# Two attention layers on one core: in layer 2, five low parts move to VectorE, the last blocks run in halves, and the score row is spread three blocks earlier

## The reference, cut to what matters

```python
def _L0_gnn_ref(xx_anchor, input, adj, weight):      # layer 1: masked attention over `input`
    anchor_adj = jnp.einsum('md,de,ne->mn', xx_anchor, weight, input)
    scores = jnp.where(adj > 0, anchor_adj, NEG_PAD)
    return jax.nn.softmax(scores / TEMPERATURE, axis=1) @ input

def _L1_gnn_ref(mole_out, adj, W, a1, a2):           # layer 2: additive attention
    Wh = mole_out @ W
    e = jax.nn.leaky_relu((Wh @ a1)[:, None] + (Wh @ a2)[None, :], negative_slope=0.2)
    att = jax.nn.softmax(jnp.where(adj > 0, e, NEG_INF), axis=1)
    return jax.nn.elu(att @ Wh)

x = _layernorm(x + _L0_gnn_ref(x, L0_gnn_input, adj, L0_gnn_weight))
x = _layernorm(x + _L1_gnn_ref(x, adj, L1_gnn_W, L1_gnn_a1, L1_gnn_a2))
```

## Time and profile before

| | us |
|---|---|
| median of 3 runs | 1453.31 (1448.89 to 1453.78) |
| the profiled execution, whole | 1454.16 |
| its span in the trace | 1452.1 |
| PE busy | 1414.8 (97%) |
| DVE busy | 1257.9 (87%) |
| POOL busy | 1212.2 (83%) |
| ACT busy | 1069.5 (74%) |

### The profile page before, as it was taken

The page is one execution under the profiler, slowest core; times in us unless marked ns, Lnnn a source line. Parts: engine busy times, 40 slices in busy tenths (PEclk is TensorE's granted clock), DMA queues, the critical chain, the costliest instruction groups (busy, mean ns, idle before and its releaser), DMA issues.

```text
span 1452.1 us, 28336 instructions
## 1 busy us (share of the span) xinstructions
PE 1414.8 (97%) x9663; PEld 1012.1 (70%) x9663; DVE 1257.9 (87%) x2136; ACT 1069.5 (74%) x2433; POOL 1212.2 (83%) x899
## 2 busy tenths in 40 slices
PE   8899999999999999999999999979999999999995
PEld 4577777777777777777777777765666666666664
DVE  6999999999999899999999999849898898979794
ACT  6788888888888888888888888868655555545453
POOL 6788888888888888888888878738999999999995
PEclk9999999999999999999999999998999999999998
DMA  8999999999999999999999998663534343434320
GB/s 263 290 269 265 266 262 258 262 270 273 270 271 258 265 259 259 274 270 271 273 257 264 260 256 266 188 138 72 103 66 110 79 102 87 102 70 110 74 58 14
DMA packets 427918, 291.38 MB, mean 201 GB/s; under 512 B 356864, under 2 KB 403200, under 8 KB 427776
## 3 DMA queue, kind: packets, MB, share of 16 engines
q1 hardware_dynamic: 427776, 289.59, 73.0%
HBM read 160.56 MB, written 40.89 MB: 139 GB/s over the span
## 4 chain that ended last, share of the span: by engine, by line
PE 95%; DVE 3%; issue 1%; ACT 1%; DMA 0%; POOL 0%; ACTq 0%; DVEq 0%; SPq 0%; POOLq 0%
PE ps L622 17%; PE ps L708 13%; PE ps L701 12%; PE ps L648 11%; PE ps L624 9%; PE ps L661 8%; PE ps L660 8%; PE ps L659 8%; PE ps L685 6%; PE ps L592 1%; PE ps L719 1%; DVE rows L974 1%; DVE neg_mask L949 1%; PE ps L585 0%; DVE pT_lo L983 0%
## 5 line engine op out<-in xcount | busy, mean ns | idle before, releaser
L833 ACT ACTIVATE rows<-rows,exp_bias 128x512 f32<-128x512 f32 x576 | 417.6, 725 | 57.0 <-DVE exp_bias L1033 57.0
L533 POOL TENSOR_TENSOR p_lo<-p,p_hi 128x1024 fp32r<-128x1024 f32 x180 | 423.7, 2392 | 23.1 <-ACT p_hi L869 11.9
L974 DVE CUSTOM_DVE_ANT_0 rows<-ps,neg_mask 128x1024 f32<-128x1024 f32 x288 | 352.1, 1222 | 79.9 <-PE ps L661 72.5
L1068 DVE SCALAR_TENSOR_TENSOR p<-ps,e_col,edgesT 128x1024 f32<-128x1024 f32 x288 | 349.7, 1275 | 53.2 <-PE ps L678 36.7
L440 POOL TENSOR_SCALAR edges<-neg_mask 128x1536 uint8<-128x1536 bf16 x190 | 307.4, 1618 | 97.0 <-DVE neg_mask L949 85.1
L869 ACT CAST p_hi<-p 128x1024 fp32r<-128x1024 f32 x180 | 185.1, 1047 | 167.7 <-DVE p L1068 165.1
L622 PE MATMUL ps<-vals,pT_hi 128*128 128x256 f16 x1536 | 296.2, 274 | 1.4 <-ACT att L812 0.9
L819 ACT CAST pT_hi<-ps 128x512 f16<-128x512 f32 x384 | 222.8, 580 | 92.1 <-PE ps L648 91.9
L482 POOL TENSOR_TENSOR inp_sb<-rows,inp_sb 128x512 f16<-128x512 f32 x192 | 281.5, 1486 | 9.6 <-ACT inp_sb L827 1.9
L624 PE MATMUL ps<-vals,pT_lo 128*128 128x128 f16 x1536 | 275.6, 220 | 0.0
L983 DVE TENSOR_TENSOR pT_lo<-ps,pT_hi 128x512 f16<-128x512 f32 x384 | 250.7, 683 | 12.5 <-ACT pT_hi L819 12.5
(11 more groups left out here) (119 smaller groups left out, 1857.1 us busy)
## 6 DMA issues: line engine op xcount, KB each, us to landing
adj_sb<-adj SPq DMA_DIRECT2D x192, 768.0 KB, 5.4
edge_rows<-edges SPq DMA_DIRECT2D x192, 192.0 KB, 4.8
xq<-x SPq DMA_DIRECT2D x48, 64.0 KB, 2.9
xr<-x SPq DMA_DIRECT2D x48, 64.0 KB, 5.5
out<-y_w SPq DMA_DIRECT2D x5, 512.0 KB, 3.5
inp_sb<-inp SPq DMA_DIRECT2D x3, 768.0 KB, 8.2
inp_sb<-inp_sb SPq DMA_TRANSPOSE x96, 4.6
edgesT<-edge_rows SPq DMA_TRANSPOSE x48, 5.5
```

The lines of the kernel that those rows point to most:

```text
L533: nc.gpsimd.tensor_tensor(p1_lo[:, m % LO_SLOTS, :], p1[:, (NB * g + n) % P_SLOTS, :], p1_hi[:, m % HI_SLOTS, :].bitcast(F32), ALU.subtrac ...
L833: nc.scalar.activation(row_chunk(1 - par, c), row_chunk(1 - par, c), ACT.Exp, bias=exp_bias[:, 1 - par:2 - par], scale=EXP_SCALE, accum_ou ...
L974: nc.vector.tensor_tensor_reduce(row_pair(par, k), scores_pair(k), neg_mask_row[:, 2 * k * CHUNK:2 * (k + 1) * CHUNK], 1.0, -3.0e38, ALU.a ...
L1068: nc.vector.scalar_tensor_tensor(out=p1[:, (NB * g + n) % P_SLOTS, :], in0=ps[:, R_ROW:R_ROW + 2, :].rearrange("p b w -> p (b w)"), scalar ...
```

## The change

1. **Five low parts by DVE** (`DVE_LOWS` = 25, 28, 33, 38, 43, in groups 1 to 5). For these blocks ACT copies `p1` to PSUM (`copy_rows`) ahead of its high part, and DVE subtracts (`low_rows`), three blocks later in its own order (`DVE_LAG`). Block 28 was split before, with its low part on POOL; 25, 33, 38 and 43 were plain and are now split. So a group has 34 split blocks, 29 of them with POOL, and 14 plain ones. In group 0 the five blocks are plain, which makes 28 plain there. Their values are split at the end of group 0 (5 small copies on ACT, 5 small subtractions on DVE). `p1_hi` gets a sixth slot, `p1_lo` keeps its four.
2. **The last group**: blocks 44, 45 and 47 are plain (`LAST_PLAIN`), and the last six blocks are multiplied by 512 columns at a time: first all of them for the first half, then for the second. The first half is copied, turned and finished while PE makes the second.
3. **The spread** of the next group's score row stands ahead of PE's block 42 (`NB - 6`) and no longer ahead of block 45.
4. Three tiles move to the memory that layer 1 leaves free, or share it.

The diff, cut to its core:

```diff
-HI_SLOTS = 5
+HI_SLOTS = 6
 LO_SLOTS = 4
 LO_LAG = 2
-SPLITS = 30
+DVE_LOWS = (25, 28, 33, 38, 43)
+DVE_LAG = 3
+SPLITS = 29
+LAST_PLAIN = (44, 45, 47)
+HALVED = 6
...
         def split_of(n):
-            return (n * SPLITS) % NB < SPLITS
+            return (n * 30) % NB < 30 and n not in DVE_LOWS
+
+        def by_dve(g, n):
+            return g > 0 and n in DVE_LOWS
+
+        def split_in(g, n):
+            return split_of(n) and not (g == NG - 1 and n in LAST_PLAIN)
+
+        def highs_of(g):
+            return [n for n in range(NB) if split_in(g, n) or by_dve(g, n)]
...
# TensorE
             for g in range(NG):
                 after(pe, v1_set, g - 1)
-                for n in range(NB):
-                    if n == NB - 3 and g < NG - 1:
+                for n in range(NB if g < NG - 1 else NB - HALVED):
+                    if n == NB - 6 and g < NG - 1:
                         pe.wait_ge(p1_set, NB * (g + 1))
                         spread_r(g + 1)
                     products(g, n)
...
-            for w in units_of(NG - 1):
-                finish_unit(w)
+            early = len([n for n in highs_of(NG - 1) if n < NB - HALVED]) - LO_LAG
+            for i in range(2):
+                for n in range(NB - HALVED, NB):
+                    if n == NB - 1:
+                        for m in highs_of(NG - 1)[early:]:
+                            low_products(NG - 1, m, (i,))
+                    products(NG - 1, n, (i,))
+                    if i == 1 and n == NB - HALVED + 2:
+                        finish_unit(units_of(NG - 1)[0])
+            finish_unit(units_of(NG - 1)[1])
...
# ScalarE
+            def copy_rows(g, n):
+                act.wait_ge(p1_set, NB * g + n + 1)
+                after(act, dve_lo_set, dves_until(g, n))
+                act.wait_ge(v_set, g)
+                nc.scalar.copy(p1_ps, p1[:, (NB * g + n) % P_SLOTS, :]).then_inc(p1_copied, 1)
...
+            def acc_half_out(i):
+                act.wait_ge(half_done, i + 1)
...
+                nc.scalar.copy(accT[:, i * CHUNK:(i + 1) * CHUNK], acc_half((NG - 1) % 2, i)).then_inc(accT_set, 1)
...
+                    if g < NG and by_dve(g, n):
+                        copy_rows(g, n)
+                    if g < NG and (split_in(g, n) or by_dve(g, n)):
                         high_part(g, n)
...
# VectorE
+            def low_rows(g, n):
+                m = highs_until(g, n)
+                dve.wait_ge(p1_copied, dves_until(g, n) + 1)
+                dve.wait_ge(hi_set, m + 1)
+                after(dve, lo_used, m + 1 - LO_SLOTS)
+                nc.vector.tensor_tensor(p1_lo[:, m % LO_SLOTS, :], p1_ps, p1_hi[:, m % HI_SLOTS, :].bitcast(F32),
+                                        ALU.subtract).then_inc(dve_lo_set, 1)
...
+                    if by_dve(g, n - DVE_LAG):
+                        low_rows(g, n - DVE_LAG)
```

More of the change, by code:

```diff
@@ L549, in _ @@
                 for n in range(NB):
-                    if g < NG and split_of(n):
+                    if g < NG and split_in(g, n):
                         low_part(g, n)
@@ L679, in spread_r, with low_products, products @@
                 mm.then_inc(r_ready, 1)
[L681 to L685, removed]
+            def low_products(g, n, halves=(0, 1)):
+                m = highs_until(g, n)
+                low_done(pe, g, n)
+                for i in halves:
+                    mm = nc.tensor.matmul(acc_half(g % 2, i), vals1_hi[:, values_slot(n), :],
                                           p1_lo[:, m % LO_SLOTS, i * CHUNK:(i + 1) * CHUNK], start=False,
-                                          stop=(k == SPLITS - 1))
-                mm.then_inc(lo_used, 1)
-            def products(g, n):
+                                          stop=(g < NG - 1 and n == highs_of(g)[-1]))
+                if 1 in halves:
+                    mm.then_inc(lo_used, 1)
+            def products(g, n, halves=(0, 1)):
                 if g == 0:
                     pe.wait_ge(vals1_set, n + 1)
-                if split_of(n):
-                    k = splits_before(n)
-                    m = SPLITS * g + k
+                if split_in(g, n) or by_dve(g, n):
+                    k = values_slot(n)
+                    m = highs_until(g, n)
                     pe.wait_ge(hi_set, m + 1)
@@ L698, in products @@
                         pe.wait_ge(vals1_lo_set, k + 1)
+                    if g == 1 and by_dve(g, n):
+                        pe.wait_ge(late_lo_set, dves_before(n) + 1)
                     for v in (vals1_hi, vals1_lo):
-                        for i in range(2):
+                        for i in halves:
                             mm = nc.tensor.matmul(acc_half(g % 2, i), v[:, k, :],
@@ L741, in _ @@
                     products(g, n)
-                    k = splits_before(n + 1) - 1 - LO_LAG
-                    if split_of(n) and k >= 0:
-                        low_products(g, k)
+                    k = len([m for m in highs_of(g) if m <= n]) - 1 - LO_LAG
+                    if n in highs_of(g) and k >= 0:
+                        low_products(g, highs_of(g)[k])
                     if n == 5 and g > 0:
@@ L889, in elu_parts @@
                 after(act, v_set, w if q < NG - 1 else NG - 1)
+                after(act, dve_lo_set, dves_until(q + 1, 0))
                 nc.scalar.activation(ex_rows[:, lo:hi, :], neg_w[:, lo:hi, :], ACT.Exp, scale=-1.0).then_inc(ex_set, 1)
@@ L1155, in _ @@
                         mean_steps()
+                    if by_dve(g, n - DVE_LAG):
+                        low_rows(g, n - DVE_LAG)
+                    if g == 0 and n == NB - 1:
+                        for m in DVE_LOWS:
+                            late_values_low(m)
                     if g > 0:
@@ L1164, in _ @@
                                 statistics(w)
-            for w in units_of(NG - 1):
-                denominators(w)
-                numerators(w)
-            for w in units_of(NG - 1):
-                sum_up(w)
-                statistics(w)
+            first_half, second_half = units_of(NG - 1)
+            denominators(first_half)
+            numerators(first_half)
+            sum_up(first_half)
+            denominators(second_half)
+            numerators(second_half)
+            statistics(first_half)
+            sum_up(second_half)
+            statistics(second_half)
             for w in units_of(NG - 1):
```

92 lines of the change are left out of this document (66 added, 26 removed).

## The result

The changed kernel takes 1470.22 us (median of 6 runs, 1468.01 to 1472.96), the kernel before in the same rounds 1452.01 (1448.89 to 1453.78): ratio 1.0127, 95% interval 1.0112 to 1.0141. It is **slower by 18.2 us**. The prediction was 1467.6. The profiled execution took 1468.01, its span is 1466.1.

A forecast was written before the change was run, and what follows sets the result against it. PE was taken as the bound, busy all 50 us of a window. Span 1452.1 - 5.2 + 14.4 + 2.3 + 4.8 - 2.0 = 1466.4; plus 2.06 less 0.85 gives 1467.6 us, range 1455 to 1475.

The forecast's parts named there:

- Both chains: Release sequences delaying DVE's last p1: DVE's own, PE waiting 2.3 us; a longer through POOL and ACT, 3.6 us.
- E24: The moment in a group when PE is done with block 24 and the low product behind it.
- E23: PE's end of block 23 in a group; DVE's low part of 25 starts 0.31 us behind it at the earliest.
- PE's products: PE's work in layer 2: 16 more split blocks, each saving 0.325 us, -5.2 us in all.
- stall ahead of the spread: PE waits for DVE before the next group's score row, 3.6 us in groups 1 to 4: +14.4 us.
- wait at block 31: PE waits for ACT's late high part of block 31, 0.45 us in five groups: +2.3 us (0 to 3.5).
- the clock: PE slowed to 1.2 GHz after rests, three in four, 1.2 us each for four groups: +4.8 us (0 to 13).
- the end: Last group in halves: -2.0 us (-3 to 0, if the two halves get in each other's way).
- deeper stalls: Rival: slow clock lasts twice as long, or POOL's low parts also reach PE late; 1475 us, chance 0.12.
- The gain arrives: Rival: DVE ends its 47th block before PE comes to 42, nobody waits; 1446.1 us, chance 0.09.
- Only DVE's own chain: Rival: ACT's high part of 33 is early, stalls 2.3 + 0.1 us; 1460.5, or 1455.7 without slow clock; chance 0.15.
- The stall, but no slow clock: Rival: PE waits before the spread but is not slowed behind it; 4.8 us less, 1462.8, chance 0.21.

The follow-up runs named there:

- both cures: Changed kernel with the spread ahead of block 45 again and ACT's normalisation moved from its block 30 behind its high part of 34: 1443.73 us, ratio 0.9947.
- the halved end alone: Kernel before with only the last group's halves, blocks 44, 45 and 47 plain there, no DVE low parts, spread ahead of block 45: 1450.08 us, ratio 0.9998.
- normalisation at 34: Changed kernel with ACT's normalisation of the group before moved from its block 30 behind its high part of block 34: 1459.52 us, ratio 1.0051.
- late spread: Changed kernel with the next group's score row spread ahead of block 45 again instead of 42: 1448.4 us, ratio 0.9976.
- four low parts: Changed kernel with four low parts by DVE instead of five, block 43 staying plain: 1463.2 us, ratio 1.0083.
- fifth low slot: Changed kernel with five slots for low parts instead of four, and five for high parts instead of six: 1462.48 us, ratio 1.0069.
- six low parts, normalisation at 38: Changed kernel with block 30 as sixth DVE low part, five high slots, spread ahead of block 45, ACT's normalisation at block 38: 1455.6 us, ratio 1.0019.

## Why the prediction was right

**Direction and mechanism.** The forecast was the case that happened, its time 2.6 us under the result. Part of this is luck: it forecast a loss of 14.3 us on a median of before of 1453.31, and measured are 18.2 on 1452.01. Both chains ran as laid out: from E24, predicted and measured, POOL's low part of 26 at 0.31 and 0.31, ACT free at 8.3 and 8.37, DVE's low part of 33 at 12.2 and 12.33, DVE done at 28.8 (28.7 by its own terms, 12.2 + 16.5) and 28.93. The moment at which DVE is released for 25, E23 + 0.31, was 1173.54 against 1173.24, 0.30.

**The sum, term by term.**

| term | predicted | measured | from |
|---|---|---|---|
| PE's products | -5.2 | -6.0 | 16 x 0.375, both cures against the halved end alone |
| stall ahead of the spread | +14.4 | +13.6 | the four idle times |
| wait at block 31 | +2.3 | +3.8 | plain block 30 to 35: 8.09, 7.93, 7.94, 7.93, 7.94 here, 7.20 each with both cures |
| the clock | +4.8 | +8.7 | distances, below |
| the end | -2.0 | -1.4 | 14.5 - 17.0 + 1.07 |
| sum | +14.3 | +18.7 | layer 2: +17.6 |

For the clock I take the distance from a spread to the small products of the result (L762), which PE makes after block 5 of the next group, all of it behind the rest. Here it is 21.18, 20.11, 21.24 and 20.09 us. With the normalisation at 34 it is 18.47 behind the two rests that no slow clock followed, for the same instructions. The fourth of the changed kernel (its spread is shown above), then the fourth of that other kernel:

```profile
1383.99 2.04 PE L762 MATMUL ps<-w_c,accT 128*128 128x129 f32 x16
```

```profile
1357.43 1.09 PE L712 MATMUL ps<-ident,r_col 128*128 128x128 f32 x8 [2.52 <-DVE p L1148]
...
1375.90 2.04 PE L762 MATMUL ps<-w_c,accT 128*128 128x129 f32 x16
```

So the four spells cost 2.7, 1.6, 2.8 and 1.6. The late spread gives a check: it takes away stall and clock and lets POOL be late, by 0.8 us in all (the stretches from spread to small products against those with both cures), which is 13.6 + 8.7 - 0.8 = 21.5 us, and it gave 1470.2 - 1448.4 = 21.8. The table has 1.1 over 17.6. In this execution group 0 was short: from its spread to the next it took 70.17 us (974.35 to 1044.52), and 71.29 and 71.48 in the kernels with the normalisation at 34 and with four low parts, whose group 0 is the same code. This accounts for the rest, 1.1 to 1.3 us; why that execution was quicker there isn't shown.

The sum came out nearer than its terms, which is luck too: products and stall came out 1.6 us lower than forecast, block 31, clock and end 6.0 higher.

**Where it was off.** The mis-sized term is *The clock*, 4.8 us for the 8.7 measured. The prediction took three slow spells in four, each of 3.3 us. In this kernel all four stalls had one, and in two the clock fell during the rest, so that PE worked at half speed for 5.7 and 5.9 us. The prediction named that as the sum that is 1.8 us higher and as "deeper stalls"; the first came true, and of the second the slow clock of twice the length, in two of the four; POOL's low parts didn't reach PE late. The Trainium skill, TensorE: Matmul & The Clock Gate, "What's actually happening", has throttling as the default and activity as what lifts it. The traces agree for rests of 3.4 us, and for shorter ones only in part:

| rest of PE, us | kernel | stalls | followed by 0.50 |
|---|---|---|---|
| 3.37 to 3.41 | changed | 4 | 4 |
| 2.71 to 2.85 | fifth low slot | 4 | 3 |
| 2.52 | normalisation at 34 | 4 | 2 |
| 2.25 to 2.27 | four low parts | 4 | 2 |
| 1.77 to 1.89, ahead of a high product | six low parts, normalisation at 38 | 5 | 1 |

The wait at 31 was priced by the idle time that PE would show (0.45; the row has 0.36). The late product also lost its overlap with the one before, so the term is 2.3 for the 3.8 measured. That was a step missing from the working. The stall was 0.2 us shorter each, since block 31 made PE 0.73 later where the prediction had taken off 0.4. PE's products saved 6.0 for 5.2, since a block's split saves 0.375 and not 0.325.

**The end** was to be 13.9 us from the last product and is 14.5: ACT was still busy with the first half's exponentials when the second half's copy was due. The copy starts at 1452.31, 0.7 us behind the end of PE's last product, and before it started at once (1435.14 behind 1435.11). This is the "two halves in each other's way" of the range.

**The rivals.** "The gain arrives" needed DVE to be done before PE comes. It is what the kernel with the late spread shows, by the other way: PE comes later. "Only DVE's own chain" was measured as such with the normalisation at 34, rests of 2.52 us, 1459.5 for its 1460.5, though only two of its four rests had a slow clock behind them, where the 1460.5 pays for all. "The stall, but no slow clock" fell in this kernel.

## What to carry to other kernels

Before work is moved to an engine with slack, find the one wait in which that slack lies, and don't move the waiting point earlier in the same change: here 7.4 us of slack a group could pay for five low parts or for a spread three blocks earlier, and both together made 3.4 us of stall of them. When the bound engine must stand, count the slow clock behind the rest as well: 8.7 us on 13.6 here. A long step on a helper engine belongs where its lead on the bound engine is longest, and that place is read from the trace, since the lead may shrink along the loop.

## What the runs showed of the hardware that was not expected

- Equal rests don't cost equal time. After four rests of 2.25 to 2.27 us in one execution the granted clock was 1.00 twice and 0.50 twice. In the changed kernel a slow spell that began just after PE had started again lasted 3.4 us, and one that began during the rest lasted 6.8 (1121.8 to 1128.6 and 1282.3 to 1289.1). What sets the one or the other isn't shown by these runs.
- A product that is late by 0.36 us of visible idle time costs the path 0.6 us up to the next block and 0.7 with what follows, since the overlap with the block ahead of it is lost.
- The split of a block saves PE 0.375 us when nobody is late, more than the 0.325 read from distances in the trace before; 0.36 of it is in the rows of longer runs of split blocks.
